# A four-image block of attention, scan and experts on one core: the image loop written out, and the last image's experts and output projection arranged anew

## The reference

```python
x = x + top_k_attention(group_norm(x))        # scores 1024 x 1024, 102 largest of each row kept, softmax
t = to_tokens(x)
# two mamba passes over the tokens, forward and backward: 256 inner channels, 16 states each
t = t + (mamba_fwd(ln(ln_t(t))) + mamba_bwd(ln(ln_t(t))) + ln_t(t))
u = ln_t(t)                                   # tokens for the experts
logits = u @ router_w.T                       # 8 experts, top 2 of the softmax, weights normalized
out = u
for e in range(8):
    h = gelu(u @ w1[e] + b1[e])
    out = out + combine[:, e:e + 1] * (h @ w2[e] + b2[e])
x = from_tokens(t + out)
```

## Time and profile before

| | us |
|---|---|
| three timed executions | 1432.73, 1439.98, 1440.12 |
| median of these | 1439.98 |
| the profiled execution | 1434.79 |
| its span in the trace | 1433.0 |
| PE busy, of the span | 1257.2 (88%) |
| DVE busy | 1147.3 (80%) |
| ACT busy | 974.4 (68%) |
| POOL busy | 836.1 (58%) |

### The profile page before, as it was taken

One profiled execution on the slowest core, in us unless ns is written; L12 is line 12 of the kernel. 1 busy time (PEld: TensorE's weight loads), 2 busy tenths in 40 slices (PEclk: granted clock), 3 DMA queues, 4 the chain that ended last, 5 costly groups with the idle time before them and its releaser, 6 DMA issues. The chain is left out here.

```text
span 1433.0 us, 18736 instructions
## 1 busy us (share of the span) xinstructions
PE 1257.2 (88%) x4909; PEld 677.4 (47%) x4909; DVE 1147.3 (80%) x1388; ACT 974.4 (68%) x1439; POOL 836.1 (58%) x450
## 2 busy tenths in 40 slices
PE   2609999999888989999988989999998899999967
PEld 1307345455546435445544635545464734545443
DVE  2695789998787689999688579999779578999920
ACT  1625779797655769889564677979675577979711
POOL 3022389798152369889235258879617138979915
PEclk9859989999999989999999979999999998999979
DMA  3000123222030012222022012222103011322203
GB/s 81 15 0 2 33 68 108 87 90 89 16 116 18 32 47 98 93 89 103 17 73 76 1 48 75 109 81 102 60 1 118 16 33 62 113 85 93 89 1 132
DMA packets 30509, 92.02 MB, mean 64 GB/s; under 512 B 4790, under 2 KB 8764, under 8 KB 30428
## 3 DMA queue, kind: packets, MB, share of 16 engines
q1 hardware_dynamic: 30428, 91.10, 18.5%
HBM read 88.34 MB, written 2.75 MB: 64 GB/s over the span
## 5 line engine op out<-in xcount | busy, mean ns | idle before, releaser
L669 POOL TENSOR_TENSOR work<-expo,ring 128x1024 f32<-128x1024 f32 x128 | 300.4, 2367 | 108.4 <-DVE expo L1393 107.8
L669 POOL TENSOR_TENSOR ring<-ring 128x1024 f32<-128x1024 f32 x128 | 300.2, 2367 | 28.1 <-DVE ring L1393 28.1
L1393 DVE TENSOR_TENSOR_SCAN ring<-ring,ps 128x1024 f32<-128x1024 f32 x128 | 284.8, 2263 | 7.9 <-PE ps L1823 4.1
L1393 DVE TENSOR_TENSOR_SCAN expo<-ring,ps 128x1024 f32<-128x1024 f32 x128 | 285.6, 2270 | 0.0
L1870 PE MATMUL ps<-ring,ident 128*128 128x512 f32 x512 | 247.8, 604 | 4.7 <-POOL ring L669 3.7
L1870 PE MATMUL ps<-work,ident 128*128 128x512 f32 x512 | 250.4, 596 | 0.8
L724 ACT ACTIVATE b_dtx_tok<-dtx_tok,b_tok 128x256 f32<-128x256 f32 x448 | 189.3, 493 | 0.0
L958 ACT ACTIVATE ring<-dt_f,decay 128x1024 f32<-128x1024 f32 x128 | 147.1, 1149 | 55.1 <-DVE expo L1393 32.7
L1870 PEld LDWEIGHTS ps<-ring,ident 128*128 128x128 f32 x512 | 88.1, 190 | 114.6 <-POOL ring L669 58.6
L1823 PEld LDWEIGHTS ps<-ident,b_dtx_tok 128*128 128x128 f32 x896 | 100.8, 141 | 75.4 <-DVE expo L1393 39.6
L1823 PE MATMUL ps<-ident,b_dtx_tok 128*128 128x128 f32 x896 | 119.0, 276 | 5.2 <-DVE expo L1393 4.9
(11 more groups left out here) (283 smaller groups left out, 2187.4 us busy)
## 6 DMA issues: line engine op xcount, KB each, us to landing
ring<-c_rows SPq DMA_DIRECT2D x128, 512.0 KB, 3.6
b_dtx_tok<-comb_rows SPq DMA_DIRECT2D x16, 512.0 KB, 4.2
dtx_tok<-comb_rows SPq DMA_DIRECT2D x16, 512.0 KB, 5.5
x_c<-in_x SPq DMA_DIRECT2D x4, 512.0 KB, 3.3
out<-xs_f SPq DMA_DIRECT2D x4, 512.0 KB, 2.7
w<-in_L_ffn_w SPq DMA_DIRECT2D x2, 512.0 KB
ring<-in_L_attn_f_in_proj_w SPq DMA_DIRECT2D x1, 256.0 KB
ring<-in_L_attn_b_in_proj_w SPq DMA_DIRECT2D x1, 256.0 KB
```

The costliest lines, as they stand in the source:

```text
L669: pool.tensor_tensor(hc[odd][:, k, :], hs[odd][:, k, :], c_all[:, odd, :], ALU.mult).then_inc(hc_ready, 1)
L1393: v.tensor_tensor_scan(hs[odd][:, k, order], dA[:, k, order], dbu[:, order], 0.0, ALU.mult, ALU.add).then_inc(scan_ready, 1)
```

## The change

Five things are changed.

1. The hardware loops over images on all five engines become loops of the generator, so the program holds each image written out. The image number is a constant in every wait. The short loops over states stay.
2. The output projection of the last image goes by blocks (`last_project_out`): one block is 8 products. It writes to `ps23`, whose two banks are first cleared by a product with a row of zeros (`pick`, bf16), and accumulates. The forward direction's two blocks stand ahead of the last two `add`s of the backward direction, and each backward block waits for its own gate. DVE adds the residual from `ps23`.
3. The normalized tokens `en` of the last image: tiles 0 to 3 on POOL, 4 to 7 on DVE. PE waits for each half apart.
4. The experts of the last image (`last_experts`): ACT writes each expert's activation to a buffer of its own, a slot of `ring` (`late_act`), so gelu waits for no selection. SP reads all eight weight rows back to back into eight buffers (`late_rows`). Selections of even experts are on DVE and of odd ones on POOL, in four buffers (`late_sel_e`); the wait for a buffer is `expert_added` of expert x-4. PE does all eight hidden layers, then bias and identity products, and then the eight additions in a row. ACT's copy of the transposed weights comes after gelu 2 instead of gelu 1.
5. The result of the last image is copied and stored by halves of 512 columns, the first after the last expert's first half.

The diff, cut to its core:

```diff
@@ sync @@
+            def load_last_weights(m):
+                sp.wait_ge(comb_copied, m + 1)
+                sp.dma_start(comb_rows[:, :], comb_t).then_inc(comb_stored, 16)
+                sp.wait_ge(comb_stored, 16 * (m + 1))
+                passed(sp)
+                for x in range(EXPERTS):
+                    sp.dma_start(late_rows[x], comb_rows[x:x + 1, :].to_broadcast([P, N])).then_inc(
+                        weight_loaded[x] if x < 4 else late_loaded[x - 4], 16)
...
-            with sp.Fori(1, BATCH - 1) as b:
+            for b in range(1, BATCH - 1):
                 sp_image(b, b - 1, b + 1)
...
+        def wait_for_last(eng, m, x):
+            if x < 4:
+                eng.wait_ge(weight_loaded[x], 4 * EXPERTS * m + 16)
+            else:
+                eng.wait_ge(late_loaded[x - 4], 16)
+            eng.wait_ge(late_gelu, x + 1)
+            eng.wait_ge(expert_added, m * EXPERTS + max(x - 3, 0))
@@ gpsimd @@
-            with pool.Fori(1, BATCH - 1) as b:
+            for b in range(1, BATCH - 1):
                 pool_image(b, b - 1, b + 1)
             pool_image(BATCH - 1, BATCH - 2)
             expert_deviation(BATCH - 1)
-            expert_norm(BATCH - 1)
-            for x in range(EXPERTS):
-                select(BATCH - 1, x)
+            pool.wait_ge(ln3_coef, BATCH)
+            for i in range(TILES // 2):
+                pool.tensor_scalar(en[:, i, :], t2[:, i, :], ln_rstd[:, i:i + 1], xh_bias[:, i:i + 1],
+                                   ALU.mult, ALU.add).then_inc(en_ready, 1)
+            for x in range(1, EXPERTS, 2):
+                wait_for_last(pool, BATCH - 1, x)
+                pool.tensor_tensor(late_sel_e[x % 4], late_act[x], late_rows[x], ALU.mult).then_inc(late_sel[1], 1)
@@ scalar @@
-            with act.Fori(1, BATCH) as b:
+            for b in range(1, BATCH):
                 act_image(b, b - 1)
...
+            for x in range(3):
+                last_gelu(m, x)
+            router_copies(m)
+            for x in range(3, EXPERTS):
+                last_gelu(m, x)
+            act.wait_ge(out_stored, 16 * m)
+            for h in range(HALVES):
+                act.wait_ge(expert_added, (m + 1) * EXPERTS + h)
+                copy(halves(out_c)[h], halves(ps01)[h]).then_inc(out_copied, 1)
@@ vector @@
-            with dve.Fori(1, BATCH - 1) as b:
+            for b in range(1, BATCH - 1):
                 dve_image(b, b - 1, b + 1)
...
-            add_residual(m)
+            add_residual(m, ps23)
...
+            for i in range(TILES // 2, TILES):
+                v.tensor_scalar(en[:, i, :], t2[:, i, :], ln_rstd[:, i:i + 1], xh_bias[:, i:i + 1],
+                                ALU.mult, ALU.add).then_inc(en_late, 1)
...
+            for x in range(0, EXPERTS, 2):
+                wait_for_last(dve, m, x)
+                v.tensor_tensor(late_sel_e[x % 4], late_act[x], late_rows[x], ALU.mult).then_inc(late_sel[0], 1)
@@ tensor @@
-            with pe.Fori(1, BATCH - 1) as b:
+            for b in range(1, BATCH - 1):
                 pe_image(b, b - 1, b + 1)
...
+            def last_project_out(m, d, k):
+                pe.wait_ge(gated, DIRS * BLOCKS * m + 2 * d + k + 1)
+                pe.wait_ge(scan_ready, UNITS * (m + 1) - 1)
+                if d + k == 0:
+                    for h in range(HALVES):
+                        mm(halves(ps23)[h], pick[0:1, 1, :], pick[0:1, 0:BANK // P, :].rearrange("p s m -> p (s m)"),
+                           start=True, stop=False)
+                for i in range(TILES):
+                    last = mm(ps23[:, i * P:(i + 1) * P], gate[:, d, k, i * P:(i + 1) * P],
+                              outproj_t[:, d, k, :], start=False, ...
...
-            add(m, 1, PAIRS - 1, 1, stop=True)
-            project_out(m)
-            expert_input(m)
+            for d, k in ((0, 0), (0, 1)):
+                last_project_out(m, d, k)
+            for k in range(BLOCKS):
+                add(m, 1, PAIRS - 1, 1, [k], stop=True)
+            for k in range(BLOCKS):
+                last_project_out(m, 1, k)
+            last_expert_input(m)
             route(m)
-            experts(m)
+            last_experts(m)
```

82 lines of the change are left out of this document (70 added, 12 removed).

## The result

The changed kernel takes 1423.98 us, the median of 7 executions (1419.5 to 1427.93). The kernel before, timed beside it, takes 1438.05 us, also the median of 7 (1432.73 to 1440.12). The ratio is 0.9897, with a 95% interval of 0.9878 to 0.9916: 14.8 us less, between 12 and 17.5. The forecast was 1424. Two later comparisons of the same two kernels gave 0.9918 and 0.9917 (experiments 6), so 12 to 15 us is the size of the gain.

A forecast was written before the change was run, and what follows sets the result against it. Bounds: ACT's and PE's jumps back at image boundaries, and PE from the last image's router on. Terms 3.3 + 1.2 + 1.4 + 0.3 + 6.6 = 12.8 us off 1436.9 give 1424 us, range 1414 to 1434.

The forecast's parts named there:

- Boundaries: Last decay to row maxima between images: written out, all three are entered like the first, saving 3.3 us.
- register arithmetic: Waits depending on the image number become constants: 0.4 us in each of three score stages, 1.2 us.
- Projection: Last image's output projection by blocks, half of it ahead of the last two additions: 1.4 us saved.
- Tokens in two halves: POOL and DVE each make half the normalized tokens, removing at most PE's 0.54 us wait: 0.3 us taken.
- Experts: Last image's experts: PE ends 6.0 us earlier, halved final copy and transfer give 0.6, together 6.6 us.
- The turns: DVE and POOL selections take turns, 3.57 us a pair against 3.44 for PE's two additions; 2.6 us slack, no cost.
- PE's last addition: Sign of being right: it ends 9 to 10 us before the span's end does now, relative to the last state.
- The level: Starting time of the kernel before, the mean of its four times shown: 1436.9 us.
- (a): Rival: in the last image's experts, selections or their rows become the bound; 1427 us, chance 0.14.
- (b): Rival: written-out image loops give nothing, something else ending an image is as late; 1428.6 us, chance 0.11.
- (c): Rival: other stages of the middle images gain by constants, PE's half-clock intervals shorten; 16.8 us saved, 1420, chance 0.09.
- (d): Rival, slower: eight short state-loop jumps on PE cost 3.4 us each in written-out code; 1451 us, chance 0.04.

The follow-up runs named there:

- experiments 6: Changed kernel unaltered, timed twice more against the kernel before: 1427.01 us, ratio 0.9918, and 1425.41 us, ratio 0.9917.
- experiments 2: Kernel before with the image loop written out on ACT alone or PE alone: second boundary 26.85 or 27.01 us, against 28.14.
- tail_only: Changed kernel with the five image loops put back: 1430.76 us, ratio 0.9948 against the kernel before.
- after_again: Changed kernel unaltered, timed a second time beside the kernel before: 1427.01 us, ratio 0.9918.
- experiments 3: Changed kernel with all eight selections on POOL or all on DVE: 1421.34 or 1430.38 us, one execution each; tails 66.30 and 66.25, against 66.64.

## Why the prediction was right

**Boundaries, forecast 3.3 us, and register arithmetic, 1.2.** Together 4.57 were measured. Three causes were separated by experiments 2: ACT's jump, PE's jump at the second boundary, and PE's waits with registers in the first two score steps. With all of them in, the second boundary's 2.6 are 1.65 up to the scaled input, 0.66 from there to the first score tile and 0.33 in the score steps; PE's jump alone would cost 1.0. The prediction took the last as 0.4 in each of three score stages. It is 0.42 and 0.33 for images 1 and 2, and nothing for image 3, which the earlier trace rows show at 17.49 already. The sum is right all the same, since the jumps were measured against a first boundary that held 0.42 of it: the third boundary gave 1.53, all of it ACT's jump, for 1.1 + 0.4. The scans gained nothing. They take 184.4 us in each image of the changed kernel, and 184.2, 184.2 and 182.7 in the one before, the last with 10.2 us at half the clock and the others with 13.7. At 13.7 us the images inside the image loops take 184.1 to 184.2 in the traces of all kernels that have these loops, and the written-out ones 184.4 throughout: written out they are 0.25 us slower, and neither ACT's loop nor PE's alone accounts for it. In the attention stretch of image 2 something may have been gained. With half clock at nearly the same places it took 130.09 us in the loop (before) and 128.7 to 129.2 written out, 126.21 (tail_only) and 125.3 to 125.7 written out. No run isolates this.

**Projection, forecast 1.4 us.** 1.2 at the residual. The bank clearing took 0.60 for the estimated 0.5, and a pause of 0.30 stands before the second half, where the sum had 0.1 between the additions alone.

**Tokens in two halves, forecast 0.3.** 0.8 from residual to router. The term was sized by PE's wait of 0.54 alone. But the halves now end together and PE makes its eight transposes back to back in 1.94 us; before, there were two groups of 1.08 and 1.12 with the wait between, 2.75 from start to end. The engines didn't hinder each other much: POOL 1.86 us for four tiles, against half of 3.45.

**Experts, forecast 6.6 with the end.** From hidden layer 3 to PE's end 5.8 for 6.0: 28.16 us against a sum of 27.9. From PE's end to the span's end 1.0 for 0.6: ACT had copied the first half before PE was done, and only one small copy and one half transfer are left. ACT's two copies and the transfers:

```profile
1416.12 0.60 ACT L764 ACTIVATE xs_f<-ps 128x512 f32<-128x512 f32 x1 [17.50 <-PE ps L2169]
1416.74 1.14 SPq L508 DMA_DIRECT2D out<-xs_f  x2
1416.91 0.60 ACT L764 ACTIVATE xs_f<-ps 128x512 f32<-128x512 f32 x1 [0.20 <-PE ps L2169]
```

The turns came as foreseen (up to 3.13 us) and cost nothing, also as foreseen. The pause before the first addition took the 3.4 us at half the clock with it. The half clock from the transposes on, of which the prediction said that it stays, did stay, for 13.7 us instead of 17.1 (in after_again 17.1, with a tail of 66.84). Between the two parts, from the router to hidden layer 3, 11.74 us are left of 11.95. One of the signs listed doesn't follow from the forecast: PE's last addition was to end "9 to 10 us before the span's end does now", but the sum puts it 75.7 - (71.5 - 7.7) = 11.9 before, and 12.2 were measured.

**The level.** 1436.9 was taken for the kernel before; its median in the comparison is 1438.05. The level was 1.2 too low and the gain, 14.1 by the two medians, 1.3 larger than the sum, so the two errors cancel, and that the time was met to a tenth of a microsecond is luck. Whether that 1.3 is more than the scatter can't be said: the spans differ by 13.0, and the later comparisons give 12.

**The rivals.** (a) falls with experiments 3: even all eight on POOL cost 0.25 us. (b) falls with the boundaries. (c): over the whole execution PE was at half the clock for 164.6 us before and 164.8 after, since other stretches had more of what the tail lost; what constants may have given elsewhere is at most the microsecond in image 2. (d), the slower one, falls: the state loops in the written-out code leave an image's scans at 184.4 us, the same at every place and 0.25 more than before, where 3.4 us for each jump were feared. The Trainium skill's rule on a jump out of the fetched pages ("Runtime: NRT & Kernel Launch", Instruction fetch mechanics) fits the long jumps, 1.6 us on ACT, and the missing cost of the short ones; which jumps leave the fetched pages and what the fetch itself takes no run here shows.

## What to carry to other kernels

A jump back of a long hardware loop is seen as idle time right before the head of the next pass, once with no releaser (`issue`) and once put down to a product of PE, and is worth writing out when that head is on the critical path; short inner loops may stay. Before work is shared between two engines, ask who waits for it: here buffers and an order on PE that keeps it fed, taken together, were all of the gain, and one engine would have done the selections. When parts of a percent are at stake, compare milestones between the same two points in the traces, not spans, since executions of one kernel that differ in PE's half-clock time differ by more than such an edit brings.

## What the runs showed of the hardware

**How the half clock spreads over an execution.** In the 42 images 1 to 3 of the fourteen traces, the attention stretch goes with the time that PE spent in it at half the clock: 6.8 us give 125.3 to 126.2 us, 10.2 give 126.8 to 127.7, 13.7 give 127.8 to 130.1, 17.1 give 129.9 to 130.8, 20.5 give 131.0 to 131.6. That is some 0.4 us for each at half the clock, with up to 2.3 us between images of the same amount. An image's scans show the same, 182.4 to 182.9 at 10.2 us and 184.1 to 184.4 at 13.7. The same code gets 6.8 in one execution and 20.5 in the next. The 28 runs of the changed kernel agree: the six with a mean granted clock of 0.942 or more took 1418.6 to 1422.3 us, the six with 0.936 or less 1426.0 to 1431.5. It is a relation; that the clock makes the length was not tried in these stretches.

**Needless products.** In the tail nine of them, 7.9 us of PE time, took the half clock from 13.7 us to 3.4 and gave 2.95 us; eight, in a single trace, left 6.8 and gave 1.3. PE had been idle 8.3 us there before. Ahead of the first image's transposes 43 more products were worth 1.2 us where the clock stayed full up to the transposes, and nothing in the trace where it fell at the last.
